# A graph layer on one core: GpSimd waits for the pair before to land at each pair's first gather, and widens 16 index columns there

## The chip, the core and the metric

The kernel runs on one core of a Trainium2 chip. Its time is the device time of one execution, in microseconds. The profile comes from one further execution, taken by the hardware profiler. The engines are named as in the profile: PE is TensorE's matmuls, PEld its weight loads, DVE is VectorE, ACT is ScalarE, POOL is GpSimd, and SP is SyncE, which only issues transfers here.

## What is computed

A layer over a graph of 12500 nodes with 256 features and 212500 edges (100000 random pairs in both directions, and a loop at each node, sorted by destination). All numbers are float32.

```python
edge_index = jnp.stack([src, dst])
xn = _layernorm(x, axis=-1)
x = x + gnn(xn, W1, b1, W2, b2, edge_index) + mix(xn[None], W_qk, b_qk, W_v, b_v, gamma, beta)[0]
x = x + ffn(_layernorm(x, axis=-1)[None], ...)[0]

def gcn_conv(x, W, b, src, dst, num_nodes):   # twice in gnn, 256 to 128 and 128 to 256, relu between
    h = x @ W
    # self loops are added to src and dst as s and d, deg = edges into each node
    norm = dinv[s] * dinv[d]                  # dinv = deg ** -0.5
    msg = h[s] * norm[:, None]
    return jax.ops.segment_sum(msg, d, num_segments=num_nodes) + b
```

`mix` is an attention without a softmax over pairs of nodes: keys are normalised over all nodes, multiplied with the values into a 256 x 256 matrix, and that is applied to the queries. `ffn` is a two-layer GELU network whose result is used for the half of the nodes with the largest routing weight.

## The kernel before, in words

Both graph convolutions are done alike. A table in device memory holds one row of 128 numbers for each node. The edges lie in 1661 chunks of 128; a chunk is one gather (128 rows of 512 bytes, one to each partition) and one product on TensorE: a 0/1 matrix S, which says which of 128 nodes each edge ends at, times the gathered rows. Eight chunks are a half, two halves are a pair, and there are 104 pairs in each of the two layers (the last pair has 13 chunks).

GpSimd issues the gathers, in an order that is written out without a loop (`gather_layer`, the gather itself is L551). They go into a ring of 32 places, that is two pairs: the halves of even pairs into quarters 0 and 1, those of odd pairs into quarters 2 and 3. Ahead of a half, GpSimd waits until the same half of the pair before last has been summed (`s_sum[layer][h]`). It reads the row numbers of a chunk from a column of `idx_now`, a buffer of two sets of 64 int32 columns. `next_indices` (the cast, L538) fills one set, that is four pairs, from the 16-bit columns `src_idx`; it runs once in four pairs, behind the gathers of the second pair of a set, and one more time ahead of each layer.

TensorE sums a half into one bank (`sum_half`, L834). It waits for two gathers at a time (`s_gath[quarter][k // 2]`), and for S of that half (`s_S`). Between chunks it does other work in fixed places: in layer 1 the mixer, one step in two pairs (L856, L864, L873, L881), in layer 2 the feed-forward network (L975, L985, L998 and others). VectorE adds the sum to the accumulator (L1306), builds S for a pair to come (L1295), finishes tiles of layer 1 (L1344, L1346) and does its parts of the mixer (L1357 to L1373) and the network. ScalarE moves results out of the banks (L627 to L639 in layer 1). TensorE, VectorE, ScalarE and SyncE run these stages in loops. Layer 1 stands from 178 to 2557 us of the span, layer 2 from 2570 to 5017.

Of the kernel before, what the change touches and what calls it, by code (L numbers as in the profile page):

```python
# [20 lines left out]
def gps_layer_kernel(nc, x, src, dst, W1, b1, W2, b2, W_qk, b_qk, W_v, b_v, gamma, beta, attention_mask, wr, br,  # L21
# [16 lines left out]
    HALF = 8  # L38
    PAIR = 2 * HALF
    PAIRS = 4 * math.ceil(math.ceil(E / (PAIR * P)) / 4)  # L40
# [9 lines left out]
    SETS = 4  # L50
# [4 lines left out]
    LAST_CHUNKS = math.ceil(EDGES_IN_LAST / P)  # L55
# [18 lines left out]
    with ctx:  # L74
# [3 lines left out]
        def sem(name):  # L78
            return ctx.enter_context(nc.semaphore(name))
# [9 lines left out]
        src_idx = indices[:, 0:CHUNKS // 2].bitcast(i16)  # L89
        dst_of = indices[:, CHUNKS // 2:CHUNKS].bitcast(i16)  # L90
        idx_now = indices[:, CHUNKS:CHUNKS + 2 * SETS * PAIR].bitcast(i32).rearrange("p (a c) -> p a c", a=2)
# [210 lines left out]
        s_idx = sem("indices_ready")  # L302
# [5 lines left out]
        s_gath = [[sem(f"gathered{h}_{k}") for k in range(HALF // 2)] for h in range(4)]  # L308
        s_S = [[sem(f"S_ready{i}_{h}") for h in range(2)] for i in range(2)]
        s_sum = [[sem(f"visit_summed{i}_{h}") for h in range(2)] for i in range(2)]  # L310
# [71 lines left out]
        def control_words(engine_type, g, first, n):  # L382
            _, words = nc.values_load_multi_w_load_instructions(  # L383
                ctl[0:1, ds(g, 1), first:first + n].rearrange("p a c -> p (a c)"), engines=[engine_type], min_val=0,
                max_val=(1 << 31) - 1, skip_runtime_bounds_check_because=own_table)
            return words
# [118 lines left out]
        def _(pool):  # L505
# [28 lines left out]

            sets = PAIRS // SETS

            def next_indices(gg):
                pool.tensor_copy(idx_now[:, gg % 2, :], src_idx[:, gg * SETS * PAIR:(gg + 1) * SETS * PAIR])\  # L538
                    .then_inc(s_idx, 1)

            def gather_layer(layer):
                for gg in range(sets):
                    pool.wait_ge(s_idx, layer * sets + gg + 1)
                    for i in range(SETS):
                        for h in range(2):
                            pool.wait_ge(s_sum[layer][h], gg * SETS + i + 1)
                            quarter = 2 * (i % 2) + h
                            real = HALF if gg * SETS + i < PAIRS - 1 else min(HALF, LAST_CHUNKS - h * HALF)
                            for k in range(real):
                                c = i * PAIR + h * HALF + k  # L550
                                pool.indirect_dma_start(  # L551
                                    ring[:, quarter * HALF + k, :], None, table[layer],
                                    bass.IndirectOffsetOnAxis(ap=idx_now[:, gg % 2, c:c + 1], axis=0),
                                ).then_inc(s_gath[quarter][k // 2], 16)
                        if i == 1 and gg + 1 < sets:
                            next_indices(gg + 1)

            pool.wait_ge(s_eTe, 2 * (PAIR // 4))
            next_indices(0)
            pool.wait_ge(s_tab1, 16 * len(TABLE1_PARTS))  # L560
            gather_layer(0)
            next_indices(0)
            pool.wait_ge(s_tab2, 16 * TILES)
            gather_layer(1)
            pool.wait_ge(s_sum[1][0], PAIRS + 2)
            pool.memset(x_end, 0.0).then_inc(s_tail_zero, 1)
# [135 lines left out]
        def _(pe):  # L702
# [57 lines left out]
            def first_columns(g):  # L760
                first = g * UNITS // 2
                n = ((g + 1) * UNITS - 1) // 2 - first + 1
                _, words = nc.values_load_multi_w_load_instructions(
                    cols_row[0:1, first:first + n], engines=[mybir.EngineType.PE], min_val=0, max_val=(1 << 31) - 1)
                cols = []
                for w in words:
                    w = pe.snap(w)
                    for col in (w & 0xFFF, w >> 12):
                        cols.append(pe.snap(nc.s_assert_within(
                            pe.snap(col), 0, SUBS * TILES - 1,  # L770
                            skip_runtime_bounds_check_because="the kernel's own table of columns holds no other")))
                return cols[g * UNITS % 2:]
# [910 lines left out]
```

## Time and profile before

| | us |
|---|---|
| median of the three timed runs | 5187.69 |
| lowest and highest | 5187.25, 5188.09 |
| the profiled execution | 5153.4 |
| its span, first to last instruction | 5151.5 |

| engine | busy us | share of the span |
|---|---|---|
| POOL | 3210.2 | 62% |
| PE | 2670.3 | 52% |
| PEld | 2310.7 | 45% |
| DVE | 1500.2 | 29% |
| ACT | 791.8 | 15% |

All numbers of the rows come from the profiled execution. Busy time doesn't count the sequencers' own instructions (registers, branches, waits), so an engine that is slow at these shows as idle, with "issue" as the reason. "Remote" is a wait whose end the profile can't put down to a particular instruction. The mean granted clock of TensorE was 0.724 of full speed.

### The profile page before, as it was taken

How to read it: one execution, taken by the hardware profiler on the slowest of the kernel's cores; microseconds unless marked ns; L12 is line 12 of the kernel's file. 1: busy time of each engine (PE TensorE's matmuls, PEld its weight loads, DVE VectorE, ACT ScalarE, POOL GpSimd, SP SyncE). 2: the span in 40 equal slices, each digit the busy share in tenths (PEclk: the TensorE clock that was granted, in tenths of full speed). 3: DMA queues.
4: the chain of work that ended last, by engine and by line, in shares of the span. 5: the costliest groups of instructions: out<-in, count | busy, mean ns of one | idle time of the engine just before them, and what ended most of it. 6: DMA issues, size and time to landing. Idle time of an engine off the chain costs nothing.

```text
span 5151.5 us, 53481 instructions
## 1 busy us (share of the span) xinstructions
PE 2670.3 (52%) x14390; PEld 2310.7 (45%) x14391; DVE 1500.2 (29%) x3686; ACT 791.8 (15%) x1584; POOL 3210.2 (62%) x3395
## 2 busy tenths in 40 slices
PE   6534434443343334333336756666657666665663
PEld 6433323333333333333325545555546555554562
DVE  7222222222222222222212323233223332332336
ACT  2301101110110111110001212112212121221222
POOL 0466666666666666666666666666666666666650
PEclk9766666666666666666557878778888777887886
DMA  4211111111111111111211111111111111111116
GB/s 135 70 48 50 48 49 48 49 48 49 48 48 49 48 49 48 49 48 49 62 51 49 50 48 50 48 51 51 49 49 51 50 50 49 51 49 52 48 47 206
DMA packets 190681, 288.68 MB, mean 56 GB/s; under 512 B 58778, under 2 KB 136982, under 8 KB 190392
## 3 DMA queue, kind: packets, MB, share of 16 engines
q0 software_dynamic: 106304, 217.92, 16.2%
q1 hardware_dynamic: 80326, 66.01, 4.2%
q10 hardware_dynamic: 3968, 3.80, 0.2%
q8 instruction: 32, 0.52, 0.0%
q14 instruction: 51, 0.42, 0.0%
HBM read 249.02 MB, written 38.49 MB: 56 GB/s over the span
## 4 chain that ended last, share of the span: by engine, by line
another core or an unknown queue 44%; issue 20%; PE 13%; DVE 10%; DVEq 8%; ACT 5%; DMA 0%; ACTq 0%; POOL 0%; SPq 0%; POOLq 0%
PE bank L985 4%; PE bank L998 3%; PE bank L834 2%; DVEq L383 2%; DVE arena L1295 2%; DVEq L1306 1%; DVE acc L1306 1%; DVEq L1295 1%; DVEq L1538 1%; ACT arena L679 1%; PE bank L881 1%; DVEq L1531 1%; PE bank L755 1%; PE bank L864 1%
## 5 line engine op out<-in xcount | busy, mean ns | idle before, releaser
L551 POOL DMA_INDIRECT arena<-table,indices x3322 | 3189.9, 960 | 1779.8 <-issue 942.5
L834 PE MATMUL bank<-arena 128*128 128x128 f32 x6644 | 1108.5, 320 | 508.8 <-issue 330.9
L834 PEld LDWEIGHTS bank<-arena 128*128 128x128 f32 x6644 | 1047.5, 233 | 575.9 <-issue 426.7
L1306 DVE SCALAR_TENSOR_TENSOR acc<-bank,folded,acc 128x128 f32 x832 | 254.9, 347 | 2058.3 <-remote 1748.4
L1295 DVE SCALAR_TENSOR_TENSOR arena<-indices,base_col,bank 128x1024 f32 (+1 forms) x416 | 532.2, 1280 | 176.5 <-issue 98.9
L985 PE MATMUL bank<-arena 128*128 128x256 f32 x1568 | 464.1, 457 | 134.6 <-issue 98.3
L985 PEld LDWEIGHTS bank<-arena 128*128 128x128 f32 x1568 | 359.0, 235 | 214.6 <-issue 116.2
L998 PE MATMUL bank<-arena 128*128 128x256 f32 x1376 | 372.1, 416 | 39.9 <-issue 28.3
L881 PE MATMUL bank<-arena 128*128 128x256 f32 x392 | 161.4, 584 | 409.4 <-ACT arena L639 267.8
L864 PE MATMUL bank<-arena 128*128 128x256 f32 x392 | 168.2, 574 | 386.8 <-ACT arena L631 296.3
L998 PEld LDWEIGHTS bank<-arena 128*128 128x128 f32 x1376 | 280.6, 211 | 99.2 <-issue 45.7
L881 PEld LDWEIGHTS bank<-arena 128*128 128x128 f32 x392 | 113.6, 305 | 439.8 <-ACT arena L639 272.5
L864 PEld LDWEIGHTS bank<-arena 128*128 128x128 f32 x392 | 104.6, 295 | 412.9 <-ACT arena L631 305.8
L679 ACT ACTIVATE arena<-bank,fb1col 128x256 f32<-128x256 f32 x344 | 134.9, 477 | 649.5 <-remote 498.9
L873 PE MATMUL bank<-ident,arena 128*128 128x128 f32 x196 | 46.4, 380 | 305.6 <-issue 175.9
L975 PE MATMUL bank<-ident,arena 128*128 128x128 f32 x196 | 45.0, 371 | 297.1 <-DVE arena L1497 261.7
L873 PEld LDWEIGHTS bank<-ident,arena 128*128 128x128 f32 x196 | 29.7, 189 | 328.4 <-issue 192.6
L975 PEld LDWEIGHTS bank<-ident,arena 128*128 128x128 f32 x196 | 28.8, 184 | 307.1 <-DVE arena L1497 269.4
L965 PE MATMUL bank<-folded,arena 128*128 128x256 f32 x196 | 78.8, 491 | 121.1 <-ACT arena L668 103.6
L1357 DVE TENSOR_REDUCE sm<-bank 128x2 f32<-128x512 f32 (+1 forms) x49 | 33.8, 690 | 338.3 <-remote 266.1
L1517 DVE TENSOR_TENSOR xs<-bank,fb2row 128x256 f32 (+1 forms) x98 | 37.1, 420 | 300.1 <-remote 151.6
L667 ACT ACTIVATE arena<-bank 128x256 f32<-128x256 f32 x49 | 18.9, 385 | 676.3 <-remote 483.7
(270 smaller groups left out, 2248.5 us busy)
## 6 DMA issues: line engine op xcount, KB each, us to landing
arena<-table,indices POOLq DMA_INDIRECT x3322
base_rows<-xs SPq DMA_DIRECT2D x49, 256.0 KB
xs<-in_x_dram SPq DMA_DIRECT2D x6, 1792.0 KB, 16.8
table<-acc SPq DMA_DIRECT2D x98, 64.0 KB
acc<-base_rows SPq DMA_DIRECT2D x7, 896.0 KB, 12.0
out_dram<-acc SPq DMA_DIRECT2D x7, 896.0 KB, 5.0
table<-acc SPq DMA_DIRECT2D x6, 896.0 KB, 4.6
arena<-base_rows SPq DMA_DIRECT2D x5, 896.0 KB, 10.0
```

The source lines that it names most:

```text
L383: _, words = nc.values_load_multi_w_load_instructions(ctl[0:1, ds(g, 1), first:first + n].rearrange("p a c -> p (a c)"), engines=[engine_t ...
L551: pool.indirect_dma_start(ring[:, quarter * HALF + k, :], None, table[layer], bass.IndirectOffsetOnAxis(ap=idx_now[:, gg % 2, c:c + 1], ax ...
L679: last = act.activation(H_of(k, two), pH[k // 2][:, (k % 2) * 2 * P:(k % 2 + 1) * 2 * P], ACT.Gelu_apprx_tanh, bias=fb1col[:, k:k + 1])
L834: last = nc.tensor.matmul(visit_sum(layer, par, h), S_of(layer, par, h)[:, k, :], ring[:, quarter * HALF + k, :], start=(k == 0), stop=(k ...
L864: last = nc.tensor.matmul(pK[:, 2 * e * P:2 * (e + 1) * P], Wk[:, k, e * P:(e + 1) * P], xT[:, k, :], start=(k == 0), stop=(k == KD - 1))
L873: last = nc.tensor.transpose(pE[:, (j * KD + k) * P:(j * KD + k + 1) * P], ET[:, k, j * P:(j + 1) * P], ident[:, :])
L881: last = nc.tensor.matmul(pG[:, k * D:(k + 1) * D], En[:, j, k, :], xn[:, j, :], start=(j == 0), stop=(j == 1))
L965: nc.tensor.matmul(pY1[:, j * D:(j + 1) * D], aggT[:, j * P:(j + 1) * P], gW2[:, :], start=True, stop=False)
L985: last = nc.tensor.matmul(pH[h // 2][:, (h % 2) * 2 * P:(h % 2 + 1) * 2 * P], fw1[:, k, h * P:(h + 1) * P], lnT[:, k, :], start=(k == 0), ...
L998: last = nc.tensor.matmul(pY[j][:, 0:D], H_of(h, two)[:, j * P:(j + 1) * P], fw2[:, h, :], start=(h == 0), stop=(h == KH - 1))
L1295: return dve.scalar_tensor_tensor(S_of(layer, par, h), bc(dst_of[:, ds(g * PAIR + h * HALF, HALF)].rearrange("p (c a) -> p c a", a=1), [P, ...
L1306: last = dve.scalar_tensor_tensor(a, visit_sum(layer, par, h), mask[:, ds(turn, 1)], a, ALU.mult, ALU.add)
```

## The change

`next_indices` goes. In its place `widen` casts any range of columns of one set and raises its semaphore by the number of columns. `all_landed` makes GpSimd wait for the last gather of a given pair: the semaphore of that pair's second half and last two places, at the count that all gathers so far give it. At the start of each pair but a layer's first, GpSimd now waits for the pair before (`all_landed`), then casts 16 columns of the next set (`widen`), then goes on to the pair's first half as before. The last set of a layer has no next one, and there the wait stands without the cast.

```diff
-            def next_indices(gg):
-                pool.tensor_copy(idx_now[:, gg % 2, :], src_idx[:, gg * SETS * PAIR:(gg + 1) * SETS * PAIR])\
-                    .then_inc(s_idx, 1)
+            def widen(gg, first, past):
+                pool.tensor_copy(idx_now[:, gg % 2, first:past],
+                                 src_idx[:, gg * SETS * PAIR + first:gg * SETS * PAIR + past]).then_inc(s_idx, past - first)
+
+            def all_landed(layer, g):
+                quarter = 2 * (g % 2) + 1
+                left_out = [c for c in (PAIR - 2, PAIR - 1) if c >= LAST_CHUNKS]
+                pool.wait_ge(s_gath[quarter][HALF // 2 - 1],
+                             32 * (layer * (PAIRS // 2) + g // 2 + 1) - (16 * len(left_out) * layer if g % 2 else 0))
 
             def gather_layer(layer):
                 for gg in range(sets):
-                    pool.wait_ge(s_idx, layer * sets + gg + 1)
+                    pool.wait_ge(s_idx, (layer * sets + gg + 1) * SETS * PAIR)
                     for i in range(SETS):
+                        g = gg * SETS + i
+                        if g > 0:
+                            all_landed(layer, g - 1)
+                        if gg + 1 < sets:
+                            widen(gg + 1, i * PAIR, (i + 1) * PAIR)
                         for h in range(2):
-                            pool.wait_ge(s_sum[layer][h], gg * SETS + i + 1)
+                            pool.wait_ge(s_sum[layer][h], g + 1)
...
-                        if i == 1 and gg + 1 < sets:
-                            next_indices(gg + 1)
```

On GpSimd, the first three pairs of layer 1 stand so before. A name in brackets is what the instruction waits for; `visit_summed0_0` is `s_sum[0][0]`, and a row with x7 stands for seven gathers.

```order
L551 DMA arena<-table,indices 128x128 [waits visit_summed0_0,indices_ready,table1_written]
L551 DMA arena<-table,indices 128x128 x7
L551 DMA arena<-table,indices 128x128 [waits visit_summed0_1]
L551 DMA arena<-table,indices 128x128 x7
L551 DMA arena<-table,indices 128x128 [waits visit_summed0_0]
L551 DMA arena<-table,indices 128x128 x7
L551 DMA arena<-table,indices 128x128 [waits visit_summed0_1]
L551 DMA arena<-table,indices 128x128 x7
L538 CAST indices<-indices 128x64
L551 DMA arena<-table,indices 128x128 [waits visit_summed0_0]
L551 DMA arena<-table,indices 128x128 x7
```

The same place in the changed kernel, where `gathered1_3` is the last semaphore of an even pair and `gathered3_3` that of an odd one:

```order
L538 CAST indices<-indices 128x16 [waits indices_ready,table1_written]
L562 DMA arena<-table,indices 128x128 [waits visit_summed0_0]
L562 DMA arena<-table,indices 128x128 x7
L562 DMA arena<-table,indices 128x128 [waits visit_summed0_1]
L562 DMA arena<-table,indices 128x128 x7
L538 CAST indices<-indices 128x16 [waits gathered1_3]
L562 DMA arena<-table,indices 128x128 [waits visit_summed0_0]
L562 DMA arena<-table,indices 128x128 x7
L562 DMA arena<-table,indices 128x128 [waits visit_summed0_1]
L562 DMA arena<-table,indices 128x128 x7
L538 CAST indices<-indices 128x16 [waits gathered3_3]
L562 DMA arena<-table,indices 128x128 [waits visit_summed0_0]
```

The cast of 64 columns between the second and the third pair became one of 16 ahead of each pair, and each but the first waits for a landing. The other engines' instructions stand as before.

## Rows read from the trace of the kernel before

**Rows 1.** The page: busy time, and the group of the gathers.

```profile
PE 2670.3 (52%) x14390; PEld 2310.7 (45%) x14391; DVE 1500.2 (29%) x3686; ACT 791.8 (15%) x1584; POOL 3210.2 (62%) x3395
...
L551 POOL DMA_INDIRECT arena<-table,indices x3322 | 3189.9, 960 | 1779.8 <-issue 942.5 <-remote 567.3 <-DVEq L1291 151.0
```

**Rows 2.** Timeline, GpSimd at a cast: start, us, engine, line, operation [idle before].

```profile
1046.43 0.26 POOL L538 CAST indices<-indices 128x64 int32<-128x64 int16 x1
1046.86 0.97 POOL L551 DMA_INDIRECT arena<-table,indices  x1 [0.17 <-issue]
```

**Rows 3.** Waits of GpSimd in layer 1 and layer 2: us, times, longest.

```profile
POOL arena L551 <- remote: 299.2, 88, 5.5
...
POOL arena L551 <- remote: 268.0, 110, 5.7
POOL arena L551 <- PE bank L834: 98.0, 30, 6.5
```

**Rows 4.** Timeline, GpSimd in layer 1: gathers behind stalls.

```profile
853.91 0.95 POOL L551 DMA_INDIRECT arena<-table,indices  x1 [3.59 <-remote]
...
899.41 0.95 POOL L551 DMA_INDIRECT arena<-table,indices  x1 [5.38 <-remote]
...
922.33 0.95 POOL L551 DMA_INDIRECT arena<-table,indices  x1 [3.06 <-remote]
...
956.68 0.96 POOL L551 DMA_INDIRECT arena<-table,indices  x1 [4.19 <-remote]
```

**Rows 5.** Timeline, the start of layer 1: a gather and TensorE's sum.

```profile
184.71 0.95 POOL L551 DMA_INDIRECT arena<-table,indices  x1 [0.30 <-issue]
187.23 1.23 PE L834 MATMUL bank<-arena 128*128 128x128 f32 x4 [1.20 <-DMA arena<-table,indices]
```

**Rows 6.** Busy time by stretch: us; PE, PEld, DVE, ACT, POOL; clock, DMA, GB/s.

```profile
942.30:952.50 10.20, 0.00 (x0) 0.00 (x0) 2.24 (x4) 0.00 (x0) 7.89 (x9) 0.50 0.20 51
956.70:966.00 9.30, 7.89 (x44) 6.98 (x44) 5.20 (x12) 1.39 (x6) 7.17 (x8) 0.80 0.18 46
```

**Rows 7.** Timeline, VectorE at the first scaling of two pairs.

```profile
925.85 0.35 DVE L1344 SCALAR_TENSOR_TENSOR acc<-acc,dinv,b1row 128x128 f32 x1 [0.73 <-issue]
...
952.03 0.35 DVE L1344 SCALAR_TENSOR_TENSOR acc<-acc,dinv,b1row 128x128 f32 x1 [7.01 <-issue]
```

**Rows 8.** Timeline, GpSimd and TensorE at the end of layer 1.

```profile
2515.35 0.95 POOL L551 DMA_INDIRECT arena<-table,indices  x1 [5.24 <-remote]
...
2550.65 0.95 POOL L551 DMA_INDIRECT arena<-table,indices  x1 [0.30 <-issue]
...
2553.49 0.37 PE L834 MATMUL bank<-arena 128*128 128x128 f32 x1 [1.74 <-issue]
...
2556.28 3.99 PE L834 MATMUL bank<-arena 128*128 128x128 f32 x17 [0.33 <-issue]
```

**Rows 9.** Timeline, GpSimd in layer 2: two stalls, 8 gathers before each.

```profile
3014.91 0.95 POOL L551 DMA_INDIRECT arena<-table,indices  x1 [1.93 <-remote]
...
3026.67 0.95 POOL L551 DMA_INDIRECT arena<-table,indices  x1 [1.99 <-remote]
```

**Rows 10.** Timeline, GpSimd: three stalls with 16 and 8 gathers between.

```profile
796.17 0.95 POOL L551 DMA_INDIRECT arena<-table,indices  x1 [2.92 <-remote]
...
816.76 0.95 POOL L551 DMA_INDIRECT arena<-table,indices  x1 [0.69 <-remote]
...
830.46 0.95 POOL L551 DMA_INDIRECT arena<-table,indices  x1 [3.92 <-remote]
```

**Rows 11.** Timeline, GpSimd: the first and the last stalled start of a pair.

```profile
246.07 0.95 POOL L551 DMA_INDIRECT arena<-table,indices  x1 [3.73 <-remote]
...
4969.09 0.95 POOL L551 DMA_INDIRECT arena<-table,indices  x1 [4.54 <-PE bank L834]
```

**Rows 12.** Busy time of the stretch of layer 2, columns as in rows 6.

```profile
2569.87:5010.00 2440.13, 1551.84 (x7301) 1320.83 (x7302) 714.94 (x1597) 453.03 (x794) 1609.47 (x1686) 0.78 0.19 51
```

**Rows 13.** The page's DMA queues, one of two for instructions: packets, MB, share.

```profile
q14 instruction: 51, 0.42, 0.0%
```

More of the change, by code:

```diff
@@ L535, in _ @@
             sets = PAIRS // SETS
-            def next_indices(gg):
-                pool.tensor_copy(idx_now[:, gg % 2, :], src_idx[:, gg * SETS * PAIR:(gg + 1) * SETS * PAIR])\
-                    .then_inc(s_idx, 1)
+            def widen(gg, first, past):
[6 more added lines that the diff above has]
+                             32 * (layer * (PAIRS // 2) + g // 2 + 1) - (16 * len(left_out) * layer if g % 2 else 0))
             def gather_layer(layer):
                 for gg in range(sets):
-                    pool.wait_ge(s_idx, layer * sets + gg + 1)
+                    pool.wait_ge(s_idx, (layer * sets + gg + 1) * SETS * PAIR)
                     for i in range(SETS):
+                        g = gg * SETS + i
[3 more added lines that the diff above has]
+                            widen(gg + 1, i * PAIR, (i + 1) * PAIR)
                         for h in range(2):
-                            pool.wait_ge(s_sum[layer][h], gg * SETS + i + 1)
+                            pool.wait_ge(s_sum[layer][h], g + 1)
                             quarter = 2 * (i % 2) + h
-                            real = HALF if gg * SETS + i < PAIRS - 1 else min(HALF, LAST_CHUNKS - h * HALF)
+                            real = HALF if g < PAIRS - 1 else min(HALF, LAST_CHUNKS - h * HALF)
                             for k in range(real):
@@ L554, in gather_layer @@
                                 ).then_inc(s_gath[quarter][k // 2], 16)
-                        if i == 1 and gg + 1 < sets:
-                            next_indices(gg + 1)
             pool.wait_ge(s_eTe, 2 * (PAIR // 4))
-            next_indices(0)
+            widen(0, 0, SETS * PAIR)
             pool.wait_ge(s_tab1, 16 * len(TABLE1_PARTS))
             gather_layer(0)
-            next_indices(0)
+            widen(0, 0, SETS * PAIR)
             pool.wait_ge(s_tab2, 16 * TILES)
```

## The prediction

> **What bounds the kernel now.** I read the busy table and the costliest groups first, then GpSimd's groups and waits in each of the two gather stages, then the order of time around a few of its stalls. GpSimd is the engine with the most work (62% of the span), nearly all of it 3322 gathers [rows 1]. Within a run of gathers one starts every 1.26 us: 0.95 us of instruction and 0.30 us of idle before it that the profile calls "issue" [rows 5]. 3322 x 1.26 = 4186 us of the 5151.5 us span. What remains in the two stages is stalls on GpSimd. The waits table has them under "remote" and, in layer 2, also under TensorE's bank: 88 in layer 1 with 299.2 us, 140 in layer 2 with 366.0 us [rows 3]. Each of these idle times contains the 0.30 us that every gather has, so the stalls proper are 299.2 - 26.4 = 272.8 us and 366.0 - 42.0 = 324.0 us, together 596.8 us, or 2.6 and 3.1 us per pair of 16 gathers. They stand only where the code waits for the sums of the pair before last (the ring holds two pairs), at a pair's first or ninth gather.
>
> So GpSimd does stall for ring space. Why is TensorE more than a pair behind when data arrives quickly? The answer decides this case. At the start of layer 1, TensorE is released by the gathers themselves: the gather that starts at 184.71 ends at 185.66, and TensorE, which the profile says waited for it, starts at 187.23, 1.57 us later [rows 5]. Landing can't be the reason for a lag of a pair, some 23 us. But the three other engines crawl for part of each run. In the stretch 942.3 to 952.5, TensorE is busy 0.00 us of 10.2; in 956.7 to 966.0, right behind a stall of GpSimd, 7.89 us of 9.3 [rows 6]. VectorE takes 0.73 us to get from one pair's build to the next pair's first scaling at 925.85, and 7.01 us for the same step at 952.03, both put down to "issue" [rows 7]. The clearest place is the end of layer 1: GpSimd has issued its last gather (2550.65, ended 2551.60), which by the delay above lands at about 2553.2, and TensorE still does single matmuls with idle ahead of them (2553.49, behind 1.74 us of "issue"); only at 2556.28 does it do 17 in 3.99 us [rows 8]. The relief came 4.7 us after issue ended, behind a run of 29 gathers from 2515.35.
>
> **The law in the stalls.** The stall beyond 0.30 us follows the number of gathers since the last stall: 8 gathers before 3014.91 give 1.63 and 8 before 3026.67 give 1.69; 16 before 922.33 give 2.76; 24 before 956.68 give 3.89, or 4.15 with the cast that lies ahead of it (0.26 as in [rows 2]); 32 before 899.41 give 5.08 [rows 4, 9]. That is about 0.16 us per gather and a few tenths fixed. Partial stalls are credited: 16 gathers and a stall of 0.39 at 816.76, then 8 more and 3.62 at 830.46, together 4.01 for 24 [rows 10]. I read this as a backlog that grows by 0.16 us with every gather issued back to back, holds the other engines up, and has to empty before they run. This is inference from durations; no row names what is backed up.
>
> **The change part by part.** (1) It removes 50 of the 52 casts of 64 columns (the first of each layer stays). One stands at 1046.43 with 0.26 us, and the gather behind it is idle for 0.17 us more, in place of the usual 0.30: 0.13 us each, or 6 us, where no stall covers it [rows 2]. (2) It adds 2 x 100 casts of 16 columns. The trace has no such cast; one of four times the columns is 0.26 us [rows 2], and nothing is the lower end. I take 0.25. (3) It adds 206 waits, one at the first gather of each pair but the first, for the last gather of the pair before, which was issued just ahead. Queued behind it on GpSimd are the cast, the wait for the first half's sum and the pair's 16 gathers; TensorE waits for those only if it is less than two pairs behind. The landing costs 1.57 us from the end of the issue [rows 5]; with 0.25 for the cast and 0.17 before the next gather [rows 2], less the 0.30 that is there anyway, the forced pause is 1.7 us, and with nothing for the cast 1.44. 206 x 1.7 = 350 us. (4) No engine but GpSimd gets or loses an instruction. The index waits count columns now, and are met a pair ahead.
>
> The Trainium skill, page "DMA: Bandwidth & Descriptors", section "Anatomy of one DMA — SWDGE (gpsimd) path", fits 2.0 us plus bytes over 436 GB/s for one DMA; a gather of 64 KB would be 2.15 us from its issue, an estimate by that page, against 2.52 us in this trace (187.23 - 184.71) [rows 5]. By the page the pause would be 0.4 us shorter.
>
> **What of it lies on the path.** 350 us is less than the 596.8 us of stalls already there. Where a pair's start is stalled now (119 of 206, the first at 246.07, the last at 4969.09 [rows 11]), landing and cast are over before the sum arrives: most are of 2.7 us and more, against 1.7. They cost nothing. At the other 87 starts the pause is new: 87 x 1.7 = 148 us. By the law it is credited against the stall that follows, since the backlog drains during it as during any other. Then the sum of pauses stays 0.16 us per gather and the fixed part: a stall after 24 gathers becomes a pause of 1.7 after 16 and a stall of about 2.3 after 8 more. What is late next is the same sum of the pair before last. Splitting a stall pays the fixed part twice, 0 to 0.3 us at up to 87 places, 0 to 26 us; I take 8. The sum against the profiled execution: 5153.4 - 6 + 8 = 5155. Its own time lies 34.3 us under the median of the timed runs (5187.69), so I forecast 5190.
>
> **Rivals.**
> - *The pause frees the engines.* In these rows the crawl sets in some 6 to 10 us after a stall and not before [rows 6]. If what counts is that GpSimd is idle once every 16 gathers, however briefly, TensorE catches up, the ring is never full and only the forced pauses are left: 5190 - 8 - 596.8 + 350 = 4935; with the cast at nothing (206 x 0.26 less) 4881. For it: the runs of 24 and 32 gathers disappear, and with them the late part in which nothing moves. Against it: the end of layer 1, where landing of the last gather released nothing for three more us, and the 0.39 us stall that left its debt [rows 8, 10].
> - *The pauses come on top*: slower. If the stalls are TensorE's, ACT's and VectorE's own catching up and not a drain, and the three progress during a pause no more than during gathers, the 148 us at the unstalled starts are added: 5190 - 8 + 148 = 5330. It decides wherever a stall at the ninth gather stays as long as now behind a forced pause. For it: layer 2, where TensorE is busy 1551.84 of 2440.13 us [rows 12] and stalls repeat every 8 gathers. Against it: a ring two pairs deep passes any pause on to a later stall, as long as stalls exist.
> - *The crawl is fetching of instructions.* The Trainium skill, page "Runtime: NRT & Kernel Launch", section "Instruction fetch mechanics", says that a taken branch to a page that isn't held makes an engine wait for a DMA. These engines run loops. But the instruction queue with more packets moved 51 in the whole span [rows 13], so this has a chance near nothing here, and would give the first forecast.
> - *The waits do nothing* because landings are long past: not possible for a gather issued just ahead.
>
> **How the numbers follow.** Absorbed: 0.50, from 5130 to 5240, with a third of that within 0.2% and the rest on either side, since the layers' patterns of 8, 16 and 24 will shift. Freed: 0.30, from 4880 to 5130. On top: 0.20, from 5240 to 5350. About 0.2% (10 us) is what a measurement can tell from no change: faster 0.30 + 0.14 = 0.44, same 0.19, slower 0.20 + 0.17 = 0.37. For 8 in 10 I leave out the tenth at each end: 4925 to 5320.
>
> **What would show it.** GpSimd's stall at each pair's start never under 1.5 us. If absorbed: stalls and pauses together again about 600 us, nearly 3 us per pair, and TensorE still has stretches of 10 us at nothing. If freed: the waits for sums all but vanish, each start shows 1.7 us, TensorE's matmuls spread evenly. If on top: ninth-gather stalls of unchanged total. My forecast is wrong first if the drain isn't needed as a whole, or if the landing wait itself returns much later than that.

## The result, and the profile of the changed kernel

The changed kernel takes 5203.27 us (median of 11 runs, 5199.09 to 5208.22); the kernel before, on the same chip, 5185.88 us (11 runs, 5177.64 to 5188.09). The ratio is 1.0035, with a 95% interval of 1.0026 to 1.0044: slower by some 17 us. A second series on another chip gave 1.0031 [1.0019, 1.0043]. The profiled execution of the changed kernel has a span of 5204.4 us, near its own median, while that of the kernel before lay 32 us under its own. The 53 us between the two spans therefore overstate the change.

The page, after: the busy table, and the group of the gathers (now L562); to be read against [rows 1].

```profile
PE 2779.2 (53%) x14390; PEld 2348.0 (45%) x14391; DVE 1499.5 (29%) x3686; ACT 792.2 (15%) x1584; POOL 3238.0 (62%) x3545
...
L562 POOL DMA_INDIRECT arena<-table,indices x3322 | 3190.8, 961 | 1297.0 <-issue 988.4
```

The waits table of GpSimd, whole span (us in total, times, longest); to be read against [rows 3], whose two layers hold 299.2, 268.0 and 98.0.

```profile
POOL indices L538 <- DMA arena<-table,indices: 333.3, 193, 2.4
POOL arena L562 <- remote: 272.8, 145, 4.1
...
POOL arena L562 <- PE bank L843: 26.9, 12, 3.5
...
POOL arena L562 <- DMA arena<-table,indices: 8.9, 4, 2.7
```

The gathers take what they took (3190.8 us against 3189.9). The waits for sums fell from 665.2 us (the sum of [rows 3]) to 272.8 + 26.9 = 299.7, and 333.3 + 8.9 = 342.2 us of waits for a landing stand in their place. Together that is 23 us less than before, but the casts and the idle time behind them come on top. The timeline of GpSimd at three pair starts shows how (start, us, engine, line, operation [idle before]):

```profile
911.61 0.95 POOL L562 DMA_INDIRECT arena<-table,indices  x1 [0.30 <-issue]
914.26 0.20 POOL L538 CAST indices<-indices 128x16 int32<-128x16 int16 x1 [1.69 <-DMA arena<-table,indices]
914.92 0.96 POOL L562 DMA_INDIRECT arena<-table,indices  x1 [0.46 <-issue]
...
936.39 0.20 POOL L538 CAST indices<-indices 128x16 int32<-128x16 int16 x1 [1.61 <-DMA arena<-table,indices]
939.11 0.96 POOL L562 DMA_INDIRECT arena<-table,indices  x1 [2.52 <-remote]
...
960.70 0.20 POOL L538 CAST indices<-indices 128x16 int32<-128x16 int16 x1 [1.75 <-DMA arena<-table,indices]
962.19 0.96 POOL L562 DMA_INDIRECT arena<-table,indices  x1 [1.29 <-remote]
```

At 914.92 the sum was there already, and the pause is 1.69 + 0.20 + 0.46 - 0.30 = 2.05 us. At 939.11 it was not, and the landing lies inside a stall of 1.61 + 0.20 + 2.52 - 0.30 = 4.03 us. In the 47 us between 914.92 and 962.19 no gather but the first of a pair is delayed. The stretches of 10 us, read against [rows 6] (us; PE, PEld, DVE, ACT, POOL; clock, DMA share, GB/s):

```profile
926.30:936.40 10.10, 0.00 (x0) 0.00 (x0) 0.66 (x2) 0.00 (x0) 6.66 (x8) 0.59 0.20 52
940.00:950.00 10.00, 8.23 (x44) 7.36 (x42) 3.13 (x5) 2.38 (x3) 7.56 (x9) 0.74 0.19 52
949.00:959.00 10.00, 0.00 (x0) 0.00 (x0) 1.73 (x6) 0.00 (x0) 7.63 (x8) 0.65 0.23 59
```

TensorE still does nothing for 10 us at a time and then works off a pair. The end of layer 1 looks different from [rows 8]:

```profile
2545.82 1.22 PE L843 MATMUL bank<-arena 128*128 128x128 f32 x4 [1.34 <-DMA arena<-table,indices]
...
2550.84 1.22 PE L843 MATMUL bank<-arena 128*128 128x128 f32 x4 [1.28 <-DMA arena<-table,indices]
```

Here TensorE has caught up and is released by each landing. That alone is no effect of the change. The kernel before has such a stretch too, some 10 us ahead of its last gathers, and falls into single matmuls behind it:

```profile
2531.82 1.22 PE L834 MATMUL bank<-arena 128*128 128x128 f32 x4 [1.26 <-DMA arena<-table,indices]
...
2542.98 0.37 PE L834 MATMUL bank<-arena 128*128 128x128 f32 x1 [2.42 <-issue]
```

The second profile of the changed kernel has the single matmuls from 2530 to 2538 us, and landings behind them. Where the slow stretch lies when the layer ends differs from profile to profile.

The trace also has fewer drawn-out register, branch and semaphore instructions (over 0.30 us each; register loads from memory are not counted), which the prediction had not counted: 904 in the kernel before, 581 after. Nearly all of them are VectorE's (671 and 364) and SyncE's (220 and 200). TensorE has 11 and 14, so its slow stretches show only as "issue" ahead of single matmuls.

To compare kernels I worked two things out of each trace, and counted the drawn-out instructions. One is the time from the first to the last gather of a layer, divided by its 1660 intervals. The other is the pause on GpSimd, which is what each interval has beyond 1.26 us, apart for the first and the ninth gather of a pair.

| kernel | us per gather, layer 1 | layer 2 | pauses at the 1st, both layers | at the 9th | all pauses | drawn-out instructions |
|---|---|---|---|---|---|---|
| before | 1.429 | 1.469 | 336.0 | 279.2 | 630.0 | 904 |
| after | 1.442 | 1.489 | 539.8 | 130.7 | 683.1 | 581 |
| after, again | 1.431 | 1.473 | 522.5 | 113.6 | 646.4 | 515 |
| wait alone | 1.441 | 1.476 | 567.2 | 95.6 | 669.9 | 642 |
| casts alone | 1.427 | 1.460 | 291.8 | 304.7 | 608.9 | 884 |
| half the products | 1.419 | 1.460 | 358.7 | 227.7 | 596.8 | 1869 |
| half the bytes | 1.428 | 1.463 | 293.0 | 319.4 | 627.0 | 953 |
| half the rows | 1.432 | 1.471 | | | | 1355 |
| one small memset | 1.433 | 1.466 | 277.8 | 297.7 | 612.8 | 896 |
| two small memsets | 1.438 | 1.468 | 121.5 | 98.9 | 641.1 | 426 |
| two larger memsets | 1.486 | 1.496 | 78.9 | 49.0 | 767.5 | 16 |
| wait per half | 1.486 | 1.493 | 434.7 | 327.7 | 772.6 | 243 |
| longer pause | 1.429 | 1.482 | 552.9 | 81.5 | 646.1 | 604 |
| memsets, no wait | 1.427 | 1.474 | 428.9 | 191.3 | 630.3 | 693 |

Half the rows has no pauses in the table, since its interval without a pause is not 1.26 us. A sum of pauses leaves out intervals within a few hundredths of 1.26 us, which makes up to some 20 us. The two profiles of the changed kernel differ by 37 us in their pauses, so a single row of this table is good to some tens of us; the timed ratios carry the verdicts.

### The profile page after: what moved, and what is told of

Read it like the earlier page. It is cut to its first block, busy times and chain, and to the rows that moved or that the text cites. A ratio compares the mean times of both kernels' runs of the same rounds, so it can differ in the third digit from the quotient of the medians.

```text
span 5204.4 us, 53788 instructions
## 1 busy us (share of the span) xinstructions
PE 2779.2 (53%) x14390; PEld 2348.0 (45%) x14391; DVE 1499.5 (29%) x3686; ACT 792.2 (15%) x1584; POOL 3238.0 (62%) x3545
## 3 DMA queue, kind: packets, MB, share of 16 engines
q0 software_dynamic: 106304, 217.92, 16.0%
## 4 chain that ended last, share of the span: by engine, by line
another core or an unknown queue 36%; issue 24%; PE 13%; DVE 9%; POOL 7%; DVEq 6%; ACT 4%; DMA 1%; ACTq 0%; SPq 0%; POOLq 0%
POOL arena L562 7%; PE bank L994 3%; PE bank L1007 3%; PE bank L843 2%; DVE arena L1304 2%; DVEq L383 1%; ACT arena L688 1%; DVE acc L1315 1%; DVEq L1315 1%; DVEq L1304 1%; PE bank L873 1%; PE bank L890 1%; DVE arena L1506 1%; PE bank L789 1%
## 5 line engine op out<-in xcount | busy, mean ns | idle before, releaser
L562 POOL DMA_INDIRECT arena<-table,indices x3322 | 3190.8, 961 | 1297.0 <-issue 988.4
L843 PE MATMUL bank<-arena 128*128 128x128 f32 x6644 | 1136.3, 322 | 531.8 <-issue 319.1
L843 PEld LDWEIGHTS bank<-arena 128*128 128x128 f32 x6644 | 1056.7, 233 | 636.3 <-issue 426.2
L1007 PE MATMUL bank<-arena 128*128 128x256 f32 x1376 | 464.7, 470 | 178.6 <-issue 158.3
L994 PE MATMUL bank<-arena 128*128 128x256 f32 x1568 | 447.5, 445 | 52.9 <-issue 50.5
L1007 PEld LDWEIGHTS bank<-arena 128*128 128x128 f32 x1376 | 314.7, 237 | 285.9 <-issue 212.5
L994 PEld LDWEIGHTS bank<-arena 128*128 128x128 f32 x1568 | 346.5, 227 | 127.6 <-issue 69.0
L873 PE MATMUL bank<-arena 128*128 128x256 f32 x392 | 159.6, 550 | 401.5 <-issue 220.8
L538 POOL CAST indices<-indices 128x16 int32<-128x16 int16 (+1 forms) x202 | 40.4, 200 | 511.8 <-DMA arena<-table,indices 333.3
L890 PE MATMUL bank<-arena 128*128 128x256 f32 x392 | 155.3, 565 | 364.5 <-issue 215.3
L873 PEld LDWEIGHTS bank<-arena 128*128 128x128 f32 x392 | 101.6, 287 | 425.3 <-issue 225.9
L890 PEld LDWEIGHTS bank<-arena 128*128 128x128 f32 x392 | 109.7, 294 | 393.4 <-issue 219.9
L882 PE MATMUL bank<-ident,arena 128*128 128x128 f32 x196 | 48.6, 395 | 309.8 <-issue 191.9
L882 PEld LDWEIGHTS bank<-ident,arena 128*128 128x128 f32 x196 | 31.4, 197 | 322.1 <-issue 199.9
L974 PE MATMUL bank<-folded,arena 128*128 128x256 f32 x196 | 84.1, 520 | 116.8 <-ACT arena L677 114.5
L865 PE MATMUL bank<-ident,arena 128*128 128x128 f32 x196 | 42.9, 357 | 178.3 <-ACT arena L636 141.7
L976 PE MATMUL bank<-folded,arena 128*128 128x256 f32 x392 | 134.5, 478 | 0.0
L984 PE MATMUL bank<-ident,arena 128*128 128x128 f32 x196 | 39.4, 334 | 168.8 <-DVE arena L1506 108.3
```

What stands on the lines that cost most here:

```text
L562: pool.indirect_dma_start(ring[:, quarter * HALF + k, :], None, table[layer], bass.IndirectOffsetOnAxis(ap=idx_now[:, gg % 2, c:c + 1], ax ...
L843: last = nc.tensor.matmul(visit_sum(layer, par, h), S_of(layer, par, h)[:, k, :], ring[:, quarter * HALF + k, :], start=(k == 0), stop=(k ...
L873: last = nc.tensor.matmul(pK[:, 2 * e * P:2 * (e + 1) * P], Wk[:, k, e * P:(e + 1) * P], xT[:, k, :], start=(k == 0), stop=(k == KD - 1))
L882: last = nc.tensor.transpose(pE[:, (j * KD + k) * P:(j * KD + k + 1) * P], ET[:, k, j * P:(j + 1) * P], ident[:, :])
L890: last = nc.tensor.matmul(pG[:, k * D:(k + 1) * D], En[:, j, k, :], xn[:, j, :], start=(j == 0), stop=(j == 1))
L974: nc.tensor.matmul(pY1[:, j * D:(j + 1) * D], aggT[:, j * P:(j + 1) * P], gW2[:, :], start=True, stop=False)
```

## The experiments

The theory of the prediction is what I call the debt (A, where the expectations use letters): every gather issued back to back owes some 0.165 us, which GpSimd has to give back as idle time wherever the code lets it. Crawl is my word for stretches in which the other engines get from one instruction to the next slowly. Against it stood that TensorE's own catching up is what is waited for, that bytes or rows are what is owed, and that a pause as such, or a landing as such, does something that the total doesn't show. Each text below says which of these it weighs. All times are ratios to the kernel before on the same chip.

**The two parts of the change apart.** The waits with the old casts of 64 columns:

```diff
                     for i in range(SETS):
+                        g = gg * SETS + i
+                        if g > 0:
+                            all_landed(layer, g - 1)
...
                         if i == 1 and gg + 1 < sets:
-                            next_indices(gg + 1)
+                            widen(gg + 1, 0, SETS * PAIR)
```

> The changed kernel with the casts put back as before: one of 64 columns in four pairs, behind the second pair's gathers; the 206 waits for a landing stay. Theory A (a debt of about 0.16 us per gather has to be paid in pauses, and the waits only say where): 5186 to 5205, and if the 17 us that the change costs come from the 200 casts, within 5 us of 5186. Rival B (the landing waits themselves come on top): the 17 us stay, 5200 to 5205.

And the casts of 16 columns without the waits:

```diff
                     for i in range(SETS):
+                        if gg + 1 < sets:
+                            widen(gg + 1, i * PAIR, (i + 1) * PAIR)
...
-                        if i == 1 and gg + 1 < sets:
-                            next_indices(gg + 1)
```

> The changed kernel without the 206 waits for a landing; the casts of 16 columns at each pair's first gather stay. If the casts cost what the change costs: about 5203. If the waits do: about 5186, since a cast of 0.20 us is paid out of the debt of the pair. In the trace the stalls again stand at first and ninth gathers alike, in runs of 8, 16, 24 and 32.

The waits alone took 5188.27 us, 1.0085 [1.0071, 1.0099]; the casts alone 5133.92 us, 0.9980 [0.9971, 0.9989]. The expectations were in us of the first chip, on which 5205 us is 1.0037 of the kernel before. So the waits alone lie above what either theory had expected of them, and neither explains it. The loss is the waits', and the casts give some back: measured against the casts alone, the changed kernel is 0.5% slower. Waiting without the small casts is dearer than the whole change, though it has fewer instructions. Its timeline shows starts of two kinds, a short one (45 of 103 in layer 1 pause between 1.4 and 2.1 us), where the landing decides, and a long one (56 from 2.9 us), with two starts in between:

```profile
941.10 0.95 POOL L560 DMA_INDIRECT arena<-table,indices  x1 [3.49 <-remote]
...
960.88 0.25 POOL L538 CAST indices<-indices 128x64 int32<-128x64 int16 x1
962.66 0.96 POOL L560 DMA_INDIRECT arena<-table,indices  x1 [1.53 <-DMA arena<-table,indices]
```

The casts alone show 0.20 us of cast and 0.17 us of idle at an unstalled start, as [rows 2] had it for the larger cast:

```profile
928.56 0.20 POOL L538 CAST indices<-indices 128x16 int32<-128x16 int16 x1
928.93 0.97 POOL L560 DMA_INDIRECT arena<-table,indices  x1 [0.17 <-issue]
```

That small step at each start costs nothing, as the debt theory has it for any short pause. It does not say why the kernel becomes 10 to 13 us faster (by the ratio, by the medians); that stays open.

**Is it TensorE's catching up?** Here half of TensorE's products of the gathered rows are left out, while all gathers and the waits for them stay:

```diff
+                    if k % 2 == 0:
-                    last = nc.tensor.matmul(visit_sum(layer, par, h), ...
+                        last = nc.tensor.matmul(visit_sum(layer, par, h), ...
```

> The kernel before, with every second chunk left out of the sums on TensorE (3322 instead of 6644 matmuls and weight loads for the sums; all gathers, and the waits for all of them, stay; the result leaves out those edges). Theory A, the debt is the gathers' own: the stalls stay at 2.6 to 3.1 us per pair and the time at 5120 to 5190. Rival B, the stalls are TensorE's own catching up: it has half of its instructions for the sums, the stalls fall by half or more, and the time goes to 4600 to 4900.

It took 5124.53 us, 0.9961 [0.9946, 0.9976]. The page's group of these products went from 1108.5 us before to

```profile
L835 PE MATMUL bank<-arena 128*128 128x128 f32 x3324 | 685.0, 340 | 707.8 <-issue 435.9
```

that is, 423 us less work of TensorE on the sums brought 0.4% (20 us), although VectorE crawls more in this kernel than in any other (1597 of its 1869 drawn-out instructions are VectorE's, against 671 of 904 before). The amount of TensorE's work is not what sets GpSimd's stalls, and more than twice the drawn-out instructions on VectorE did not make the kernel slower. No run took work away from VectorE or ScalarE; what their slack was is read from a trace further down.

**Bytes or rows?** First (TensorE reads the half row twice) half the bytes of each row:

```diff
-                                    ring[:, quarter * HALF + k, :], None, table[layer],
+                                    ring[:, quarter * HALF + k, 0:F // 2], None,
+                                    table[layer].rearrange("n (a f) -> (n a) f", a=2),
```

> The kernel before, with gathers of rows of 64 numbers and not 128 (half the bytes, as many rows; TensorE reads each half row twice, so its work is the same; the result is that of other rows). If the debt follows the bytes moved: stalls fall by half or more, 4850 to 4950. If it follows the number of gathers or of rows: as before, within 1%.

It took 5145.44 us, 1.0000 [0.9990, 1.0010]. Then half the rows:

```diff
-                                    ring[:, quarter * HALF + k, :], None, table[layer],
-                                    bass.IndirectOffsetOnAxis(ap=idx_now[:, gg % 2, c:c + 1], axis=0),
+                                    ring[0:P // 2, quarter * HALF + k, :], None, table[layer],
+                                    bass.IndirectOffsetOnAxis(ap=idx_now[0:P // 2, gg % 2, c:c + 1], axis=0),
```

> The kernel before, with gathers of 64 rows of 512 bytes and not 128 (the first 64 partitions; TensorE sums over 64 partitions, with as many matmuls; the result leaves out half of the edges). If what is due for each gather goes by its rows: 0.7 to 0.9 us per gather where it is 1.43 now, 2800 to 3500 us. If it goes by the instruction, or by its 16 completions, and not by rows or bytes: it stays at about 1.43, with a shorter instruction and longer stalls, within 3% of the kernel before.

It took 5166.45 us, 1.0040 [1.0025, 1.0056]: with half the rows it isn't faster at all. The trace shows an exchange. GpSimd's timeline, its waits and the queue of the gathers on the page, with half the rows:

```profile
906.20 0.91 POOL L551 DMA_INDIRECT arena<-table,indices  x1 [0.30 <-issue]
907.41 0.91 POOL L551 DMA_INDIRECT arena<-table,indices  x1 [0.30 <-issue]
912.50 0.91 POOL L551 DMA_INDIRECT arena<-table,indices  x1 [4.19 <-remote]
```

```profile
POOL arena L551 <- remote: 680.4, 209, 8.4
POOL arena L551 <- PE bank L834: 155.7, 45, 6.3
```

```profile
q0 software_dynamic: 106304, 109.07, 9.5%
```

The interval is 1.215 us, shorter by 0.045, which is 149 us for 3322 gathers, and the waits for sums rose from 665.2 to 836.1 us, by 171. GpSimd asked faster and was made to wait longer, and the layers kept their 1.432 and 1.471 us per gather. The queue moved half the MB in the same 106304 packets, 32 per gather in all three kernels (16 with data and 16 of 4 bytes). So what is owed goes by the gather, or by these packets. Rows and bytes are excluded; these two were not told apart.

The traces hold one thing more on this. In the kernel before, the last packet of a gather ends 2.19 us after the gather's start, in the median. It is the same for the first eight gathers behind a stall (2.20 us) as for the 17th to 24th (2.19 us). The rows land on time however much is owed. What is backed up is therefore not the gathers' own transfers.

**A little time behind every gather.** Two kernels write memsets of a spare tile behind each gather, one or two of 128x8 (`spend(n)` writes n, each waiting for the one before):

```diff
                                 ).then_inc(s_gath[quarter][k // 2], 16)
+                                spend(1)
```

> The kernel before, with one memset of 8 spare columns on GpSimd behind every gather, some 0.12 to 0.2 us each, so that gathers are issued every 1.4 to 1.45 us and not 1.26. Theory A: this pays the debt of 0.16 us per gather as it arises; the stalls for the sums nearly vanish, the other engines don't crawl, and the time stays within 1% of 5186. If pauses come on top (B): 3322 times 0.15 us more, 5600 or above.

> The kernel before, with two memsets of 8 spare columns behind every gather, each waiting for the one before. One memset lay inside the 0.30 us of idle that stands before every gather, and left the gathers 1.27 us apart; two should make them 1.45 to 1.50 us apart. Theory A (0.16 us of debt per gather): this pays it as it arises. The stalls for the sums fall from some 600 us to under 150, and the time is about 3322 times the new spacing and 460 us around it, 5250 to 5450. Rival B (GpSimd's stalls are the other engines' own time and come on top): the stalls stay near 600 us, and the time is 5800 or more.

The single memset was no test: its 0.12 us lay inside the 0.30 us that GpSimd is idle between two gathers anyway, and the interval stayed at 1.27 us.

```profile
902.06 0.12 POOL L547 MEMSET spare<- 128x8 f32 x1
902.37 0.96 POOL L560 DMA_INDIRECT arena<-table,indices  x1 [0.18 <-issue]
```

It took 5159.70 us, 1.0026 [1.0014, 1.0037]; its profile, with fewer pauses than that of before, shows no reason for the 0.3%. With two, gathers start every 1.38 us, less than the 1.45 to 1.50 that the expectation had, so that its time (5250 us and more) was too long as well:

```profile
901.25 0.96 POOL L560 DMA_INDIRECT arena<-table,indices  x1
902.20 0.28 POOL L547 MEMSET spare<- 128x8 f32 x2
902.63 0.96 POOL L560 DMA_INDIRECT arena<-table,indices  x1
```

```profile
POOL arena L560 <- remote: 113.4, 77, 2.5
...
POOL arena L560 <- PE bank L844: 22.2, 11, 3.3
```

3322 x 0.12 = 399 us are added to GpSimd's path, and the kernel takes 5161.55 us, 1.0035 [1.0021, 1.0049]: 16 us more. The waits for sums fell from 665.2 to 135.6 us. It is the result on which the debt theory stands most firmly: the longer interval paid most of it, and what was left was waited for at the ring.

Then more than the debt, with two memsets of 128x48:

```diff
-        spare = sb("spare", [P, 8])
+        spare = sb("spare", [P, 48])
```

> As with the two memsets behind each gather, with 48 columns each and not 8, so that gathers are issued every 1.45 us or so, just over the 1.26 + 0.165 = 1.425 us at which the debt would be nil. Theory A: nothing is left but what layer 2's own work needs; stalls beyond the spacing under 60 us, and from here on each hundredth of a microsecond per gather costs 33 us: 3322 times the spacing and 460 us around it, about 5280 for 1.45. Rival: stalls stay at the 100 to 150 us of the narrower spacing and come on top, 5400.

Gathers start every 1.457 us, and "remote" and TensorE's bank are gone from the ring's waits:

```profile
903.97 0.96 POOL L560 DMA_INDIRECT arena<-table,indices  x1
904.93 0.35 POOL L547 MEMSET spare<- 128x48 f32 x2
905.43 0.96 POOL L560 DMA_INDIRECT arena<-table,indices  x1
```

```profile
POOL arena L560 <- DVEq L1301: 150.3, 1, 150.3
POOL arena L560 <- issue: 110.2, 172, 1.3
```

It took 5257.83 us, 1.0219 [1.0203, 1.0234]. The stretches of 10 us are even, and the other engines no longer crawl (16 drawn-out instructions):

```profile
930.00:940.00 10.00, 6.64 (x24) 5.40 (x24) 1.09 (x1) 2.23 (x3) 8.15 (x22) 0.65 0.16 39
940.00:950.00 10.00, 4.21 (x16) 3.53 (x16) 3.58 (x9) 0.14 (x1) 8.60 (x21) 0.52 0.21 53
950.00:960.00 10.00, 5.64 (x18) 3.88 (x16) 1.89 (x3) 0.60 (x1) 8.21 (x19) 0.50 0.19 46
```

The kernel before has 3.83, 0.00 and 2.97 us of TensorE in the same three stretches. The waits of TensorE and VectorE in layer 1 (200 to 2550 us) show that both have time to spare here:

```profile
PE bank L844 <- DMA arena<-table,indices: 1098.8, 681, 3.3
```

```profile
DVE acc L1316 <- PE bank L844: 1200.2, 157, 11.4
```

TensorE is released by a landing 681 times; in the kernel before it is 16 times in the same window, with 23.4 us. VectorE waits for TensorE's sums, and TensorE for the gathers. With the same work to do, neither is near its limit at 1.486 us per gather. That speaks against the rival that TensorE's or VectorE's own work simply takes 1.43 us per gather, since such an engine would be all but busy here.

Nobody waits for a sum in this kernel, the work is even, and it is the slower kernel, since GpSimd now sets the time alone. Between an interval of 1.38 us and one of 1.457 the cost goes from 0.35% to 2.2%, which agrees with 1.43 us per gather in layer 1 as the rate that can be kept up. Layer 2, with its 1.47, also loses time that isn't the debt's, and no run says what it is: here 1.496 against 1.486, with no sum late.

**Pauses of other shapes.** First the landing waited for at both halves of a pair:

```diff
                         for h in range(2):
+                            if h == 1:
+                                first_half_landed(layer, g)
```

> The changed kernel with one more wait for a landing at each pair's ninth gather, for the pair's first half (208 more waits). Theory A: pauses of 1.4 us each 8 gathers, 0.18 us per gather, pay the whole debt; stalls for sums beyond them nearly vanish in layer 1, and the time is within 1.5% of the kernel before. Rival B (the waits come on top): each of the 208 new ones adds 1.4 us where no stall stood, 5450 or more.

5282.22 us, 1.0272 [1.0255, 1.0289]. That is more than I had expected, which was up to 1.5%. The waits table has no wait for a sum left, and its timeline shows a forced pause after every 8 gathers:

```profile
905.78 0.95 POOL L567 DMA_INDIRECT arena<-table,indices  x1 [1.83 <-DMA arena<-table,indices]
...
917.16 0.20 POOL L538 CAST indices<-indices 128x16 int32<-128x16 int16 x1 [1.64 <-DMA arena<-table,indices]
917.82 0.96 POOL L567 DMA_INDIRECT arena<-table,indices  x1 [0.46 <-issue]
```

They are 1.83 - 0.30 = 1.53 and 1.64 + 0.20 + 0.46 - 0.30 = 2.00 us, and 8 gathers owe 8 x 0.165 = 1.3. (The 0.165 is the prediction's 0.16 plus the share of what it called fixed; 1.26 + 0.165 is the 1.43 of the table.) Idle time beyond the debt buys nothing: the pauses in all rose by 143 us, the time by 137.

Next a pause made longer, by four memsets behind each landing wait:

```diff
                         if g > 0:
                             all_landed(layer, g - 1)
+                            spend(4)
```

> The changed kernel with four memsets one after the other behind each landing wait, so that each pair starts with a pause of 2.5 to 3 us, as long as the mean stall. Theory A: nearly no stall at a ninth gather, starts at 2.5 to 3.3 us, time 5190 to 5300. Rival B: some 1.2 us times 206 on top of the changed kernel, 5450.

```profile
930.11 0.73 POOL L553 MEMSET spare<- 128x48 f32 x4 [1.72 <-DMA arena<-table,indices]
930.78 0.20 POOL L541 CAST indices<-indices 128x16 int32<-128x16 int16 x1
931.33 0.98 POOL L572 DMA_INDIRECT arena<-table,indices  x1 [0.36 <-remote]
```

5168.46 us, 1.0046 [1.0029, 1.0063]. 206 x 0.7 = 144 us of memsets were added to the changed kernel and cost 0.11 to 0.15% (against 1.0035 and 1.0031), inside the intervals of both. The median pause at a start is now 2.7 us in layer 1, what 16 gathers owe (16 x 0.165 = 2.6), and only two ninth gathers of that layer are still late.

And a pause without a landing, of six memsets:

```diff
                         if g > 0:
-                            all_landed(layer, g - 1)
+                            spend(6)
```

> The changed kernel with six memsets at each pair's start in place of the wait for the landing: a pause of about as long (1.3 to 1.7 us where no sum is late), with nothing waited for. If a pause costs by its length: the same time as the changed kernel, within 0.2%. If the wait for a landing itself costs (it may come back late while the other engines are held up): at or under the kernel before, 1.000.

```profile
909.21 1.13 POOL L553 MEMSET spare<- 128x48 f32 x6
910.28 0.20 POOL L541 CAST indices<-indices 128x16 int32<-128x16 int16 x1
910.63 0.98 POOL L571 DMA_INDIRECT arena<-table,indices  x1 [0.15 <-issue]
```

5152.26 us, 1.0011 [1.0002, 1.0021]. The pause came out at some 1.1 us, not the 1.5 that I had meant, so that it can't tell a landing from a pause of the same length. On the same chip it took 0.15% less than the changed kernel and 0.1% more than the kernel before, which fits neither expectation alone. It does show that 206 pauses of 1.1 us, 227 us, cost 0.1% against the kernel before and 0.3% against the casts alone.

**The changed kernel again**, on the chip of the runs with half the rows, with the larger memsets and with the pause without a landing:

> The changed kernel once more, beside the others of this group. On its first chip it took 1.0035 of the kernel before; with the casts put back it was 1.0085 on another chip, with a longer pause 1.0046. If the chip makes no difference: 1.003 to 1.004 again, and the order of the three stands. If the ratio depends on the chip: up to 1.008.

5159.88 us, 1.0031 [1.0019, 1.0043]. Its profile has 646.4 us of pauses, 16 more than that of before, where the first had 53 more. The timed difference is 17 us on the first chip; here it is 13 us by the medians and 16 by the ratio.

## Why the prediction held, and where it didn't

The forecast was 5190 us; the first comparison gave 5203. As a ratio, 5190 over the 5187.69 known then is 1.0004, against 1.0035 measured. It was inside the range, and slower by over 0.2%, the side that had a chance of 0.37, less than faster (0.44). The mechanism that I held likeliest, absorption, is the one that the runs show. One chance was miscounted: a third of 0.50 is 0.17, and the forecast says 0.19 for "same".

**The pause at each start.** Forecast: 1.7 us, and never under 1.5. The smallest is 1.48, at a start without a cast. At 103 starts the landing decided and a cast followed; they pause 2.16 us in the mean and never less than 1.96. The landing was nearly right (mostly 1.6 to 1.8 us of idle against 1.57), the cast too (0.20 against 0.25). The term that was too small is the idle time ahead of the gather behind the cast. I took 0.17 us from a row in which nothing is waited for [rows 2], and it is 0.46 or 0.48 at 99 of these 103 and 0.8 at the other four. The Trainium skill's fit of one DMA (page "DMA: Bandwidth & Descriptors", section "Anatomy of one DMA — SWDGE (gpsimd) path"), 2.15 us for these 64 KB as an estimate by that page, agrees with the end of a gather's last packet (2.19 us from the gather's start, in the median of either kernel). It falls short of what a waiter sees: from the start of the last gather at 911.61 to the cast that waited for it at 914.26 are 2.65 us.

**Absorbed.** The forced pauses were 350 us by the forecast and are some 430 as measured (206 x 2.1), against a rise of 17: that they would be set against the stalls was right. The pauses at starts grew by 204 and 187 us in the two profiles (148 forecast for the 87 new ones), and those at the ninth gather fell by 149 and 166 us. The "on top" rival priced them at an unchanged ninth; they fell by more than half, so it is out for the most part.

**The mis-sized term** is the cost of splitting a stall: 0 to 26 us, of which I took 8. Measured are 13 to 17 us in all. Two reasons offer themselves, both argued and not shown. First, the longer pause: 103 x (2.16 - 1.7) = 47 us, most of it credited again. Second, and missing in my working: paying more than is owed buys nothing. Where a stall at the ninth gather has just paid, only 8 gathers are owed at the next start, 1.3 us, and the forced 2.0 or 2.1 us are longer. The run with a wait at each half has this at every half and loses 137 us. In the first profile of the changed kernel 61 starts follow a late ninth gather and are decided by the landing. They pause 58 us beyond 8 x 0.165 each, 47 of it in layer 2. So this reason is large enough for the 17 us, and too large to be counted in full. The same count gives 35 us for the waits alone, which lost more (1.0085), so it does not put the two kernels in order. How the 17 us divide was not measured.

**The law** of 0.16 us per gather held in layer 1 in every run up to the point where it no longer bound. It was right as a rate, and is better written so: 1.43 us per gather in layer 1 whatever stands between them, from 1.419 to 1.442 in twelve of fourteen profiles; the other two are those that pause more than is owed. Layer 2 went from 1.460 to 1.489 in the same twelve, and its surplus over layer 1 is not explained by the law.

**The freed rival** had its mechanism half right and its price wrong. The changed kernel does crawl less: 904 drawn-out instructions became 581 and 515. (That TensorE is up to date at the end of layer 1 is no sign of it, as said above; my reading of [rows 8] had left out that the kernel before is up to date there until 2540 us.) With the larger memsets the crawl is gone altogether. That rival's 255 us of gain rested on the crawl being the reason why the ring is full. The runs fit a crawl that is a symptom of the same debt: whoever ends it by pausing pays the same time in pauses. The two small memsets show it: 530 us of waits gone from the table, and no time gained. What ties crawl and debt together was not found.

**The instruction fetch** had no part in it: the queue of [rows 13] moved 53 packets after, 51 before.

```profile
q14 instruction: 53, 0.43, 0.0%
```

## What to carry to other kernels

Ahead of pricing a new wait or cast on an engine that issues DMAs, divide the time of its whole run by the number of DMAs, and compare that with the interval of two that are issued back to back. If the first is longer, here 1.43 against 1.26 us, a rate may be behind the stalls. Here idle time up to the debt (0.165 us per gather) was nearly free (at most 0.5%, but 0.85% for the waits alone, which stays unexplained), and idle time beyond it cost its full length. Only fewer gathers, not smaller ones, could make such a stage shorter; so far that is argued, since no run here left gathers out. Of the kernels that leave nothing out, the casts of 16 columns without the waits are the fastest, at 0.998 of the kernel before.

## What the runs showed of the hardware

- Indirect gathers of 128 rows can be issued every 1.26 us for a while, but no kernel here kept up more than one per 1.42 us over layer 1, or per 1.46 us over layer 2. 64 rows in place of 128, or 256 bytes in place of 512 in a row, left that rate where it was (1.432 and 1.428 in layer 1).
- A gather's last packet ends 2.19 us after the gather's start, in the median, as much for the first eight behind a stall (2.20) as for the 17th to 24th (2.19). So no growing queue of these transfers stands behind the rate.
- Within a run of gathers the other engines can get from one instruction to the next slowly, while the instructions that do the work take their usual time (VectorE's L1344 takes 0.35 us in both rows): VectorE had 7.01 us of idle ahead of a step that elsewhere has 0.73 [rows 7], and has 1.14 us in the kernel with the larger memsets. No trace here shows what the engines share, if it is that.
- GpSimd executes a 0.12 us memset within the 0.30 us between two gathers, and the interval grows by 0.01 us at most (1.26 to 1.27). Two of them lengthen it to 1.38 us, two larger ones to 1.457.
- Behind a cast that waited for a landing the gather starts 0.46 to 0.48 us after the cast's end at most places; behind one that did not wait, or had memsets between the wait and itself, mostly 0.15 to 0.17.
